# Row maxima turned on VectorE in 32x32 blocks and sent to the query operand in eight pieced transfers per half

## What is computed

```python
kqv = x @ W_kqv.T
k_, q_, v_ = jnp.split(kqv, 3, axis=-1)
...
score = jnp.einsum('bhsd,bhnd->bhsn', q, k) / scale + bias[None]
attn = jax.nn.softmax(score, axis=-1)
out = jnp.einsum('bhsn,bhnd->bhsd', attn, v)
```

## Time and profile before

| | |
|---|---|
| time, median of 3 runs | 2458.93 us |
| the three runs | 2464.11, 2458.93, 2458.88 us |
| profiled execution, span from its first to its last instruction | 2465.2 us |
| its own time as a run | not listed apart; the runs lie 1.1 to 6.3 us under its span |
| PE, DVE, ACT busy, share of the span | 97%, 77%, 63% |
| attention | from about 1088 us to the end |
| length of a middle group | about 41.5 us |

### The profile page before, as it was taken

One profiled execution on the slowest core, in us unless ns is written; L12 is line 12 of the kernel. 1 busy time (PEld: TensorE's weight loads), 2 busy tenths in 40 slices (PEclk: granted clock), 3 DMA queues, 4 the chain that ended last, 5 costly groups with the idle time before them and its releaser, 6 DMA issues.

```text
span 2465.2 us, 53774 instructions
## 1 busy us (share of the span) xinstructions
PE 2399.8 (97%) x19426; PEld 1490.7 (60%) x19426; DVE 1899.4 (77%) x2889; ACT 1561.3 (63%) x3276; POOL 782.9 (32%) x901
## 2 busy tenths in 40 slices
PE   8999999996999999989999999999999999999998
PEld 7888888886999999963333333333333333333333
DVE  6666566655556555568999999999999999999994
ACT  3333333333343333315888888888888888888888
POOL 2222323225242222210113333333333333333333
PEclk9999999997999999987999999999999999999999
DMA  6999877771332222232425343434344443435321
GB/s 189 185 166 176 172 129 148 140 120 35 87 98 76 76 75 76 77 74 47 84 49 103 62 88 71 87 72 84 74 79 80 74 85 72 87 67 91 64 58 40
DMA packets 177924, 229.05 MB, mean 93 GB/s; under 512 B 42828, under 2 KB 127436, under 8 KB 177656
## 3 DMA queue, kind: packets, MB, share of 16 engines
q1 hardware_dynamic: 153048, 172.02, 37.6%
q0 software_dynamic: 22448, 50.56, 8.6%
q10 hardware_dynamic: 2176, 3.02, 0.3%
HBM read 131.47 MB, written 93.66 MB: 91 GB/s over the span
## 4 chain that ended last, share of the span: by engine, by line
PE 52%; DVE 2%; DMA 1%; ACT 0%; issue 0%; SPq 0%; DVEq 0%; ACTq 0%
PE p_o L1430 23%; PE p L1418 18%; PE p L1405 9%; PE p L1442 1%; DVE part L1255 1%; DMA q_op<-m_row 1%; PE p L1411 1%; ACT probs L1379 0%; SPq L1144 0%; ACT o_sb L1367 0%; DVE neg L1263 0%; DVE att L1282 0%; DVE att L1302 0%; ACT o_t L1357 0%; DVE rec L1279 0%
## 5 line engine op out<-in xcount | busy, mean ns | idle before, releaser
L1255 DVE TENSOR_REDUCE part<-p 128x2 f32<-128x1024 f32 x1024 | 1237.8, 1221 | 79.9 <-PE p L1405 64.8
L1379 ACT ACTIVATE probs<-p 128x512 f32<-128x512 f32 x2048 | 1109.2, 596 | 159.6 <-PE p L1418 122.8
L1405 PE MATMUL p<-k_op,q_op 50*128 50x512 f32 x2048 | 757.2, 461 | 14.0 <-DVE part L1255 10.9
L1418 PE MATMUL p<-q_op,k_op 51*128 51x512 f32 x2048 | 756.5, 451 | 1.9 <-DMA q_op<-m_row 0.7
L1430 PE MATMUL p_o<-probs,v_op 128*32 128x256 f32 x8192 | 657.4, 392 | 5.1 <-ACT o_sb L1367 1.3
L1418 PEld LDWEIGHTS p<-q_op,k_op 51*128 51x128 f32 x2048 | 312.6, 186 | 417.3 <-ACT probs L1379 355.9
L1430 PEld LDWEIGHTS p_o<-probs,v_op 128*32 128x32 f32 x8192 | 163.3, 108 | 359.7 <-ACT probs L1379 285.0
L1405 PEld LDWEIGHTS p<-k_op,q_op 50*128 50x128 f32 x2048 | 307.0, 189 | 29.3 <-DVE part L1255 26.1
L1206 POOL TENSOR_TENSOR att<-o_t,rec 128x256 f32<-128x256 f32 x63 | 39.0, 618 | 809.1 <-DVE rec L1271 809.1
L828 POOL DMA_INDIRECT xe<-xn_scratch,ids x135 | 146.3, 1083 | 340.4 <-DMA ids<-lists_scratch 309.9
L921 ACT ACTIVATE gated_e<-p_gate 128x352 f32<-128x352 f32 x135 | 62.8, 465 | 194.9 <-PE p_gate L859 115.6
(11 more groups left out here) (186 smaller groups left out, 4052.7 us busy)
## 6 DMA issues: line engine op xcount, KB each, us to landing
k_op<-qk_scratch SPq DMA_DIRECT2D x192, 128.0 KB
q_op<-qk_scratch SPq DMA_DIRECT2D x192, 128.0 KB
yr_scratch<-x SPq DMA_DIRECT2D x135, 128.0 KB
qk_scratch<-k_op SPq DMA_DIRECT2D x32, 512.0 KB
qk_scratch<-q_op SPq DMA_DIRECT2D x32, 512.0 KB
v_scratch<-v_op SPq DMA_DIRECT2D x16, 1024.0 KB
v_op<-v_scratch SPq DMA_DIRECT2D x32, 512.0 KB
x<-in_x SPq DMA_DIRECT2D x16, 512.0 KB
```

Source lines behind the costliest of these rows:

```text
L1255: v.tensor_reduce(part[c_ % 2][:, kh, :, qb], p1[use % 2][:], AX.X, ALU.max, negate=True).then_inc(s["s1_read"], 1)
L1379: a.activation(probs[kb % 4][:, h], p2[use % 3][:], ACT.Exp).then_inc(s["s2_read"], 1)
L1405: return t.matmul(p1[use % 2][:, x], q_op[u][lo:lo + S1_ROWS, pair, q0:q0 + P], k_op[u][lo:lo + S1_ROWS, pair, kh * 512:(kh + 1) * 512], s ...
L1418: t.matmul(p2[use % 3][:], k_op[u][lo:lo + S2_ROWS, pair, kb * P:(kb + 1) * P], q_op[u][lo:lo + S2_ROWS, pair, half * HQ:(half + 1) * HQ], ...
```

## The change

VectorE turns the maxima itself. `neg` becomes 128 x 32 numbers (columns 16 to 31 are zero, set once), and one DVE instruction turns each of its four 32x32 blocks within its own 32 partitions into `m_t`: partition 32b + j, column c of `m_t` is query 32b + c of column j. A row of 128 queries then lies in four pieces of 32 numbers (128 bytes), in four partitions that are 32 apart. SP sends eight transfers per half, one for each pair of heads and block b, each with eight pieces of 128 bytes, into both rows 50 and 114. PE's transposes, ACT's copies and their two slots in the score ring are gone.

```diff
-        neg = [sb(f"neg{i}", [P, 8 * PAIRS], F32R) for i in range(2)]
-        m_row = [sb(f"m_row{i}", [8 * PAIRS, P], F32R) for i in range(2)]
+        neg = [sb(f"neg{i}", [P, 32]) for i in range(2)]
+        m_t = [sb(f"m_t{i}", [P, 32]) for i in range(2)]
...
-        TURN_AT = HALF + 5
-        OWN_TURN = 5
+        TURN_AFTER = (MAX_UNITS // 2 + 1, 1)
...
+        M_LOAD = 8 * 16
...
-            def send_max(g, u, half, use):
-                sp.wait_ge(s["s2_read"], use + 4)
+            def send_max(g, u, half):
+                sp.wait_ge(s["m_t_ok"], 2 * g + half + 1)
                 for pair in range(PAIRS):
-                    for x in range(2):
-                        r = 64 * x + S2_ROWS - 1
-                        sp.dma_start(q_op[u][r:r + 1, pair, half * HQ:(half + 1) * HQ]
-                                     .rearrange("o (q c) -> o q c", q=4).bitcast(F32),
-                                     m_row[half][8 * pair + 4 * x:8 * pair + 4 * x + 4].bitcast(F32)).then_inc(m_in[half], 16)
+                    for b in range(4):
+                        j = 32 * b + 8 * pair
+                        sp.dma_start(q_op[u][S2_ROWS - 1:S2_ROWS + 64:64, pair, half * HQ:(half + 1) * HQ]
+                                     .rearrange("x (q b c) -> x q b c", q=4, b=4)[:, :, b].bitcast(F32),
+                                     m_t[half][j:j + 8]).then_inc(m_in[half], 16)
...
+            for half in range(2):
+                v.memset(neg[half][:, 16:32], 0.0).then_inc(s["neg_set"], 1)
+            dve.wait_ge(s["neg_set"], 2)
...
-                v.tensor_tensor(neg[half][:, 8 * pair:8 * pair + 8], pt[:, 0].rearrange("p x q -> p (x q)"),
-                                pt[:, 1].rearrange("p x q -> p (x q)"), ALU.min).then_inc(s["neg_ok"], 1)
+                mine = neg[half][:, 0:16].rearrange("p (j x q) -> p j x q", x=2, j=PAIRS)[:, pair]
+                v.tensor_tensor(mine, pt[:, 0], pt[:, 1], ALU.min).then_inc(s["neg_ok"], 1)
+
+            def turn_max(g, half):
+                dve.wait_ge(s["neg_ok"], g * CHUNKS + PAIRS * (half + 1))
+                if g:
+                    dve.wait_ge(m_in[half], g * M_LOAD)
+                v.transpose(m_t[half][:], neg[half][:]).then_inc(s["m_t_ok"], 1)
...
+                        if w == TURN_AFTER[0]:
+                            turn_max(g + 1, 0)
...
+                    if w == TURN_AFTER[1]:
+                        turn_max(g, 1)
...
-                    if n == OWN_TURN:
-                        row_copy(g, use + 1, 1)
-                    elif n == TURN_AT and has_next:
-                        row_copy(g + 1, use + 1, 0)
...
-                        pe.wait_ge(m_in[half], (g + 1) * (32 * PAIRS))
+                        pe.wait_ge(m_in[half], (g + 1) * M_LOAD)
...
-                        if n == TURN_AT:
-                            turn_max(g + 1, 0, use + 1)
-                    if n == OWN_TURN:
-                        turn_max(g, 1, use + 1)
```

More of the change, by code:

```diff
@@ L1080, in attend @@
         p_o = ps("p_o", [P, HQ])
-        names = ("passed ones_in init s1_ps s1_read neg_ok s2_ps s2_read pv_done pv_side o_ok rec_ok "
+        names = ("passed ones_in init neg_set m_t_ok s1_ps s1_read neg_ok s2_ps s2_read pv_done pv_side o_ok rec_ok "
                  "pool_c o_st0 o_st1 att_ok o_out base_in0 base_in1 yg_in0 yg_in1 fin_base fin_y "
@@ L1104, in turns_at @@
         def turns_at(g):
-            out = [OWN_TURN] + [h * HALF + OUT_TURN for h in range(2) if g or h]
-            return sorted(out + ([TURN_AT] if g < GROUPS - 1 else []))
+            return [h * HALF + OUT_TURN for h in range(2) if g or h]
         def use2(g, n):
-            before = 1 + sum(UNITS + len(turns_at(i)) for i in range(g))
+            before = sum(UNITS + len(turns_at(i)) for i in range(g))
             return before + n + sum(t < n for t in turns_at(g))
@@ L1160, in group @@
                     load((g + 2) % GROUPS, (u + 2) % 3)
-                send_max(g, u, 1, use2(g, OWN_TURN) + 1)
+                send_max(g, u, 1)
                 if has_next:
-                    send_max(g + 1, following(u, turn)[0], 0, use2(g, TURN_AT) + 1)
+                    send_max(g + 1, following(u, turn)[0], 0)
             groups(sp, group)
@@ L1307, in _ @@
                     join(w // CHUNK, w + 3)
+                if w == TURN_AFTER[0]:
+                    turn_max(0, 0)
             def group(g, u, turn, has_prev, has_next):
@@ L1341, in _ @@
             act.sem_inc(s["pv_done"], NK)
-            def row_copy(g, use, half):
-                act.wait_ge(s["s2_ps"], use + 1)
-                if g:
-                    act.wait_ge(m_in[half], g * (32 * PAIRS))
-                a.copy(m_row[half][:], p2[use % 3][0:8 * PAIRS, 0:P]).then_inc(s["s2_read"], 1)
             def turned_copy(g, half, use):
@@ L1367, in output_copy @@
                 a.copy(o_sb[half][:, cols], p_o[:, cols]).then_inc(s["o_ok"], 1)
-            row_copy(0, 0, 0)
             def group(g, u, turn, has_prev, has_next):
@@ L1379, in group @@
                     a.activation(probs[kb % 4][:, h], p2[use % 3][:], ACT.Exp).then_inc(s["s2_read"], 1)
-                    if n == OWN_TURN:
-                        row_copy(g, use + 1, 1)
-                    elif n == TURN_AT and has_next:
-                        row_copy(g + 1, use + 1, 0)
-                    elif n % HALF == OUT_TURN and (half or has_prev):
+                    if n % HALF == OUT_TURN and (half or has_prev):
                         turned_copy(*((g, 0) if half else (g - 1, 1)), use + 1)
@@ L1406, in max_half @@
                                 k_op[u][lo:lo + S1_ROWS, pair, kh * 512:(kh + 1) * 512], start=True, stop=True)
-            def turn_max(g, half, use):
-                pe.wait_ge(s["neg_ok"], g * CHUNKS + PAIRS * (half + 1))
-                pe.wait_ge(s["s2_read"], use + 1)
-                t.transpose(p2[use % 3][0:8 * PAIRS, 0:P], neg[half][:].bitcast(F32), ident[:]).then_inc(s["s2_ps"], 1)
             def score(u, use, n):
@@ L1450, in _ @@
                 max_half(0, w, w, 0).then_inc(s["s1_ps"], 1)
-                if w == MAX_UNITS // 2 + 2:
-                    turn_max(0, 0, 0)
             def group(g, u, turn, has_prev, has_next):
```

2 lines of the change are left out of this document (1 added, 1 removed).

## The result

The changed kernel takes 2466.85 us (median), the kernel before 2460.08 us beside it. The ratio is 1.0033, with an interval of 1.0017 to 1.0049: the change costs about 8 us. Single runs spread more than before, from 2453.4 to 2486.9 us. One run of the kernel before, at 4298 us, is left out of the ratio.

What follows compares the result with a forecast made beforehand. PE, busy 97%, was taken to bound the kernel, DVE a near second. 2465.2 - 12.7 - 0.2 + 0.2 + 9.5 = 2462.0 us; the difference, -3.2, applied to the 2458.9 median gave 2455.7, range 2447 to 2471 (8 in 10).

Steps and rivals of the forecast that it cites:

- the rival's 2466.9: At the start of half 1: small pieces cost twice 20 ns a packet, 20.7 us lost, 2466.9 us in all; chance 0.27.
- The transposes, 12.7 us less: On PE: 62 of 64 transposes stand in the open, each worth 0.205 us, so 12.7 us less.
- DVE's turn at nothing: On DVE: a turn takes 0.2 us, hidden within the 0.45 us reserve before PE wants the buffer, so it costs nothing.
- DVE as the one that holds PE: Rival, mainly at w = 17: a turn of 0.39 us exceeds DVE's reserve, some 5 us more, 2460; chance 0.08.
- The prologue's 0.2: In the prologue, where DVE sets the pace: one turn adds 0.2 us.
- The landing, 9.5 us more: At the start of half 1: maxima land 0.64 us later behind the loads, costing 9.5 us over 29 halves.
- packets of 20 ns: At the queues' end: 32 more packets per engine, on two engines, at 20 ns each, make the landing 0.64 us later.
- The step from 0.84 us to 9.5: At half 1: 0.84 us of reserve taken loses 2.96 us over nine halves, 0.33 each, 9.5 us over 29.
- The bound with 2.4 us: At half 1: if each transfer costs its queue as long as its issue, 2.4 us, 52 us are lost, giving 2498.
- sign for dear pieces: In PE's score wait for the maxima, 3.9 us before: above 17 us would mean the small pieces are dear.
- half 0's sends, "hidden too": On SP's queue: half 0's 2.4 us of extra issue time is hidden, as its maxima are used 16 us later.
- a wait of PE costs its length: At half 1's starts: lost time was counted as the waits themselves, 9.5 us, with no term for the clock.

Runs made afterwards that it cites:

- the third experiment: Kernel before, transposes and copies kept, with each half's maxima sent by eight transfers of two 512-byte pieces instead of four of four: 2464.78 us, ratio 1.0028.
- second: Changed kernel with half 1's maxima sent before the group's fifteen loads instead of behind them: 2470.65 us, ratio 1.0049.
- fifth: Changed kernel with half 1's maxima sent before the loads and GpSimd's gathers held back by about four pairs: 2445.4 us, ratio 0.9934.
- sixth: Changed kernel with half 1's maxima sent after the first six of the fifteen loads: 2458.64 us, ratio 0.9995.
- seventh: Changed kernel with half 1's maxima sent after the first six loads and half 0's turned and sent three pairs later: 2455.89 us, ratio 0.9977.
- the ninth: Changed kernel with only GpSimd's gathers held back by four pairs, half 1's sends still behind the loads: 2491.45 us, ratio 1.0128.
- the last: Changed kernel with half 0's turn one pair later (w = 18): 2478.28 us, ratio 1.0043.

## Why the prediction was wrong

The direction was wrong: 2455.7 us forecast against 2466.85. That the time lies within the range of 2447 to 2471, and close to the rival's 2466.9, is luck: neither the forecast nor that rival has the mechanism of half the loss. Step by step:

- **The transposes, 12.7 us less.** Right, a little too large: a place is worth 0.19 us in its pair (0.39 per group for two), 12.0 for all 62. The transpose's 0.205 was read from start to start; 0.02 of it is still in the pair (1.26 against 1.24).
- **DVE's turn at nothing.** Right: 0.20 us, inside the reserve; DVE as the one that holds PE did not come. The prologue's 0.2 is right too: from its first maximum to the first score 36.93 us against 36.71.
- **The landing, 9.5 us more.** Right in place and near in size: 8.1 us more excess at half 1. The landing comes 0.75 us later (1.36 - 0.61) where 0.64 was assumed, on two engines as assumed. But it was priced by packets of 20 ns, and that the size came out is luck. The packets of the changed kernel took 11 ns each, the packet sum gives the third experiment only 0.16 us (16 packets on an engine instead of 8) where 0.76 was measured, and what the runs show is a price per transfer, 0.19 us, whatever its pieces. The step from 0.84 us to 9.5 was off as well, the other way: 0.84 us taken from all 29 halves in the trace of before gives 6.6, and 0.95, the measured 0.75 and 0.20, gives 8.1. Nine halves were too few. (The bound with 2.4 us should read some 50 us by its own nine halves, not 52.) The forecast's own sign for dear pieces, a wait above 17, was met with 17.1 by the weight load's count, and yet the eight transfers of larger pieces landed just as late. The sign was badly chosen: that count was 3.9 before, when only 1.0 us was lost.
- **The step that failed: half 0's sends, "hidden too".** They were looked at for the time they have (16 us), and for that they are hidden. What they meet on the way was not looked at: GpSimd's gathers, in the same microseconds. No term stood for it, and it cost 8.3 us in 29 groups; the same meeting, of half 1's sends, took part in the last group's 2.5. The prediction removed the transpose and the copy from half 0's path without asking where its sends would then begin: 1.1 us earlier in the group, ahead of the second gather instead of with it. The second and fifth experiments show the meeting to be the cause, as only the gathers move and the ratio falls from 1.0049 to 0.9934. The sixth and seventh show it in their traces, the ninth puts it at pairs 10 to 14, and the last takes most of it away by a pair's delay.
- **The second step that failed: a wait of PE costs its length.** After some waits of 0.9 to 2.4 us, not after all, the granted clock was at half for 3 to 17 us, once for 57 us to the end, at 2.16 us a pair instead of 1.24. It adds about 3 us to the groups of the profiled execution. The spread of the runs goes with it: of the twenty, the fastest has a mean granted clock of 0.986, the slowest 0.972. In the trace of before there is no such stretch in groups 1 to 31. Its group 0 begins at half clock and shows what a pair then costs, but not that a short wait can bring it back.

Sum for groups 1 to 29: forecast -11.9 (58 x 0.205) + 9.5 = -2.4, measured +8.4.

What stays open: why engines other than SP and GpSimd start late while these two issue transfers. The traces show the late starts and the coincidence, not the resource. Whether the number of transfers or their 128-byte pieces also make it dear, beside the moment at which they begin, was not tried by itself: no run sends the old transfers 0.9 us ahead of the second gather. The seventh kernel has the same groups 1 to 29 as the fifth (1193.0 and 1192.9 us) but a median 10 us higher. Its two slowest runs have a mean granted clock of 0.972 against 0.981 to 0.984 in the others, and its last group keeps the wait for ACT; for the rest I have no account.

## What to carry to other kernels

Sending a small tile in more transfers has a price in three places: at the tail of a full queue (here 0.19 us a transfer), on engines that share no data with it when it begins just ahead of a gather of GpSimd, and in the clock after the waits that follow. A step that becomes faster also moves what it triggers. A transfer that has ample time can still be in the wrong place, so look at what every other queue issues in its microseconds, and give the small sends and the gathers separate times. When a gain is certain but the sum is not, find the waits that it creates and move their cause: here that turned +0.3% into -0.7%.

## What the runs showed of the hardware

- ACT and DVE, idle and with their inputs ready, began up to 0.83 and 0.6 us late when SP issued eight small SBUF transfers and GpSimd indirect gathers in the same 4 us, the transfers beginning 0.7 to 0.9 us ahead of the second gather. With eight such transfers beginning 0.4 us behind it, or four of larger pieces beginning with it, the loss per group was under 0.1 us.
- Transfers of 2 pieces of 512 bytes and of 8 pieces of 128 bytes landed equally late behind a full queue, in eight transfers that ran on two engines each. In a quiet queue the packets of the second took 11 ns on average.
- An issue on SP took 0.53 us for the new transfers (4.26 us for eight), against 0.61 for the old.
- The stretch at 1.2 GHz after a wait of about 0.9 us of PE was 3.4 us in one execution and over 50 in another of nearly the same kernel.
